# GpSimd's gathers of source nodes in a graph layer: the loop with staged index copies against 160 chunks written out

## The reference, cut to what matters

```python
seg = lambda v: jax.ops.segment_sum(v, dst, num_segments=n)
xs = x[src]
deg_w = jnp.maximum(seg(edge_weights), 1.0)
deg_c = jnp.maximum(seg(jnp.ones_like(edge_weights)), 1.0)
norm = edge_weights / jnp.sqrt(deg_w[src] * deg_w[dst])
gcn = seg(norm[:, None] * xs) @ Wgcn + bgcn
sage = x @ Wsage_s + seg(xs) / deg_c[:, None] @ Wsage_n + bsage
agg_w = seg(edge_weights[:, None] * xs)
gin = ((1.0 + gin_eps) * x + agg_w) @ Wgin + bgin
gconv = x @ Wgc1 + agg_w @ Wgc2 + bgc
eop = seg(edge_weights[:, None] * jax.nn.relu(xs + edge_attr)) @ Wedge + bedge
ops = jnp.stack([gcn, sage, gin, gconv, eop])
...
x = _layernorm(x + jnp.einsum('k,knd->nd', weights, ops), axis=-1)
```

## Time and profile before

| | us |
|---|---|
| median of 3 runs | 2110.08 |
| lowest and highest run | 2105.61, 2110.34 |
| span of the profiled execution | 2149.6 |

### The profile page before, as it was taken

How to read it: one execution, slowest core, us unless ns; L and a number is a source line. 1 busy time by engine, 2 the same in 40 slices (tenths; PEclk the granted TensorE clock), 3 DMA queues, 4 the chain that set the end, 5 groups by cost and what they waited for, 6 DMA issues and landing times.

```text
span 2149.6 us, 24142 instructions
## 1 busy us (share of the span) xinstructions
PE 1612.0 (75%) x6229; PEld 1037.0 (48%) x6229; DVE 949.9 (44%) x2579; ACT 868.5 (40%) x1181; POOL 1416.1 (66%) x1730
## 2 busy tenths in 40 slices
PE   2006577688889888888888988978988888888435
PEld 1005567545445454555455545545545455445335
DVE  7882465534334343443244433433435253334325
ACT  3784333334434252543254433533435253344003
POOL 6673766676676667667767666666666666666761
PEclk9999865889999899999899998989989999999757
DMA  5111433322222222222222222221222222212421
GB/s 98 25 25 46 132 106 100 83 44 47 58 51 61 48 47 58 52 48 58 44 66 49 55 60 44 54 51 43 68 48 47 54 57 47 59 43 56 103 44 37
DMA packets 81242, 124.52 MB, mean 58 GB/s; under 512 B 28856, under 2 KB 30631, under 8 KB 80009
## 3 DMA queue, kind: packets, MB, share of 16 engines
q0 software_dynamic: 44544, 48.32, 13.4%
q1 hardware_dynamic: 34966, 74.37, 10.9%
q10 hardware_dynamic: 1650, 1.04, 0.2%
HBM read 120.23 MB, written 3.40 MB: 58 GB/s over the span
## 4 chain that ended last, share of the span: by engine, by line
PE 40%; issue 20%; another core or an unknown queue 17%; DVE 11%; ACT 6%; POOL 3%; DVEq 2%; DMA 0%; POOLq 0%; SPq 0%; ACTq 0%
PE psum L1276 26%; PE psum L1257 11%; ACT ring L606 4%; POOL ring L564 3%; DVE ring L1072 2%; DVE sums L1061 2%; DVE early L986 1%; ACT early_x L687 1%; DVE attr L951 1%; DVE early L990 1%; PE psum L1308 1%; PE psum L1337 1%; PE psum L1338 1%; DVEq L1061 1%
## 5 line engine op out<-in xcount | busy, mean ns | idle before, releaser
L564 POOL DMA_INDIRECT ring<-node_table,idx x1280 | 1239.5, 968 | 612.4 <-issue 505.3
L1276 PE MATMUL psum<-table_sb,early_x 128*128 128x455 f32 x2464 | 1040.0, 572 | 46.5 <-issue 33.3
L1276 PEld LDWEIGHTS psum<-table_sb,early_x 128*128 128x128 f32 x2464 | 479.4, 200 | 531.2 <-issue 516.4
L1257 PE MATMUL psum<-ring 128*128 128x120 f32 x2560 | 412.5, 316 | 225.2 <-DVE ring L1072 104.7
L1257 PEld LDWEIGHTS psum<-ring 128*128 128x128 f32 x2560 | 378.3, 226 | 289.8 <-issue 160.1
L687 ACT ACTIVATE early_x<-early,minus_ids 128x256 f32<-128x256 f16 x616 | 408.1, 746 | 239.2 <-remote 144.6
L986 DVE TENSOR_TENSOR early<-psum,digit_hot 128x455 f32<-128x455 f32 x176 | 111.0, 631 | 885.4 <-remote 580.8
L678 ACT ACTIVATE early<-early 128x256 f32<-128x256 f32 x44 | 18.3, 416 | 523.4 <-DVE early L1007 305.0
L653 ACT ACTIVATE ring<-attr 128x512 f32<-128x512 f32 x160 | 99.6, 623 | 319.2 <-DVE attr L951 230.6
L690 ACT ACTIVATE early_x<-early_x,ones 128x1792 f32<-128x1792 f32 x88 | 157.4, 1789 | 2.9
L1257 PE MATMUL psum<-early 128*128 128x120 f32 x576 | 100.8, 328 | 75.8 <-issue 37.0
(11 more groups left out here) (156 smaller groups left out, 611.3 us busy)
## 6 DMA issues: line engine op xcount, KB each, us to landing
attr<-in_edge_attr SPq DMA_DIRECT2D x79, 512.0 KB
ring<-node_table,idx POOLq DMA_INDIRECT x1280
early<-in_edge_attr SPq DMA_DIRECT2D x36, 256.0 KB
src_all<-in_src SPq DMA_DIRECT2D x7, 1024.0 KB
early<-key_rows SPq DMA_DIRECT2D x11, 512.0 KB
early_x<-degree_rows SPq DMA_DIRECT2D x2, 1568.0 KB
early_x<-in_x,early_idx POOLq DMA_INDIRECT x112
node_table<-table_sb SPq DMA_DIRECT2D x1, 1666.0 KB, 6.1
```

Of the source, the lines that this page charges most:

```text
L564: nc.gpsimd.indirect_dma_start(out=feat[:, u, j, D:BLOCK], out_offset=None, in_=table, in_offset=bass.IndirectOffsetOnAxis(ap=idx[:, u, j: ...
L1257: last = nc.tensor.matmul(to[:, 0:3 * WINDOW], features[:, j, 0:2 * D], hots[:, j].rearrange("p k n -> p (k n)"), start=(j == 0), stop=(j ...
L1276: last = nc.tensor.matmul(pick_ps[k % 2].rearrange("p (b c) -> p b c", b=SPLIT), node_hot[:, k, a], table_sb[:, a * SPLIT:(a + 1) * SPLIT, ...
```

## The change

The loop over rounds becomes a Python loop over the 160 late chunks, so that the program holds every chunk's instructions in a row. Each gather names its own column of `e_src` directly. The tile `idx`, the 320 copies and the semaphore `staged` are gone. The wait for a slot's previous gathers is left out for the first four chunks, where it waited for 0. `gathers_begun` is raised once for each chunk. The other engines' programs are the same instructions with other line numbers.

```diff
-        idx = sb("idx", [P, UNROLL, TILES], U32)
-
...
-        staged = sem("staged")
...
                 pool.wait_ge(table_stored, 16)
-                with pool.Fori(0, LATE_STEPS) as i:
-                    for u in range(UNROLL):
-                        it = v * LATE + i * UNROLL + u
-                        pool.wait_ge(gathered[u], (v * LATE_STEPS + i) * (16 * TILES))
-                        for j in range(TILES):
-                            if j % HALF == 0:
-                                tiles = slice(j, j + HALF)
-                                nc.gpsimd.tensor_copy(idx[:, u, tiles], e_src[:, bass.ds(i * UNROLL + u + BASE, 1), tiles].rearrange("p c j -> p (c j)")).then_inc(staged, 1)
-                                pool.wait_ge(staged, it * 2 + j // HALF + 1)
-                                if j == 0:
-                                    pool.wait_ge(chunk_product, it + 1)
-                                pool.sem_inc(gathers_begun, 1)
-                            nc.gpsimd.indirect_dma_start(
-                                out=feat[:, u, j, D:BLOCK], out_offset=None, in_=table,
-                                in_offset=bass.IndirectOffsetOnAxis(ap=idx[:, u, j:j + 1], axis=0),
-                            ).then_inc(gathered[u], 16)
+                for c in range(LATE):
+                    u = c % UNROLL
+                    if c >= UNROLL:
+                        pool.wait_ge(gathered[u], (v * LATE_STEPS + c // UNROLL) * (16 * TILES))
+                    pool.wait_ge(chunk_product, v * LATE + c + 1)
+                    pool.sem_inc(gathers_begun, 1)
+                    for j in range(TILES):
+                        nc.gpsimd.indirect_dma_start(
+                            out=feat[:, u, j, D:BLOCK], out_offset=None, in_=table,
+                            in_offset=bass.IndirectOffsetOnAxis(ap=e_src[:, c + BASE, j:j + 1], axis=0),
+                        ).then_inc(gathered[u], 16)
```

## The result

The changed kernel takes 2156.12 us (median of four runs, 2154.0 to 2159.41); the kernel before, timed beside it, 2109.07. The ratio is 1.0228, with a 95% interval of 1.021 to 1.0246: **slower by 47 us**, where 38 us less were forecast.

What follows compares the result with a forecast made beforehand. TensorE's round with VectorE and ScalarE was taken to pace the profiled turns, GpSimd close behind and bounding the plain end. From 2110.1 us, 27.7 (24.3 + 3.4) and 10 came off: 2072.4 us, range 2025 to 2103.

Steps and rivals of the forecast that it cites:

- GpSimd's own cost of a turn: GpSimd's gathers without copies: a turn falls from 139.5 to 123 us, a chunk from 11.6 to 10.25 us.
- From the profiled execution to the timed ones: Timed turns take about 140.3 us, next to GpSimd's 139.5, so GpSimd paces at least quick ones; some 10 us gained.
- The turns: Eleven turns: GpSimd's 16.5 us saved a turn are hidden by TensorE's round at 143.9 us; worth nothing in the profiled execution.
- The plain end: Late chunks 152 to 159, bound by GpSimd: it starts at 2001.6 and ends at 2083.6 us, gaining 24.3 us.
- The factor load: Load of node factors in the plain end: holds gathers back from VectorE 20.72 us again, now at late chunk 153; no loss.
- The start of the turns: Late chunk 17: VectorE's wait of 3.43 us for gathers goes, 3.4 us gained.
- The turns are let go: Rival: GpSimd paces all timed turns, so each may fall to 135.4 us; 27.7 + 54 off, 2028 us; chance 0.26.
- Slower, by the clock: Rival: shifted work lowers TensorE's clock in the turns, some 10 us each; 2122 us with five such turns; slower: chance 0.06.
- By the code: Rival: reading in the straight program costs time, slower or level; chances 0.06 for slower, 0.08 for level.
- the gathers are not quicker: Rival: a gather indexed from the big table costs 0.17 us more, eating the 1.4 us a chunk; 2110 us; level: chance 0.08.
- The factor load takes the gain of the end: Rival: GpSimd stands still during the factor load in the plain end, losing 20.7 us; 2093 us; chance 0.10.

Runs made afterwards that it cites:

- again: The kernel before, unchanged, run once more for a profile: 2111.68 us, ratio 1.0001; profiled span 2104.2 us.
- late_paused: Changed kernel with an unused copy and its wait ahead of each four gathers from late chunk 4 on: 2129.88 us, ratio 1.0074.
- start_paused: Changed kernel with an unused copy and its wait ahead of each four gathers in late chunks 0 to 3 alone: 2142.70 us, ratio 1.0129.
- the execution shown ahead: The kernel before, unchanged, in the profile shown ahead of the prediction: span 2149.6 us.
- straight_copies: Kernel before with late gathers written out chunk by chunk, copies into the index tile and their waits kept: 2110.11 us, ratio 0.9998.
- dummy_copies: Changed kernel with an unused copy and its wait ahead of each four gathers throughout: 2112.64 us, ratio 1.0007.

## Why the prediction was wrong, point by point

- **GpSimd's own cost of a turn**: right. The unhindered chunks at the start take 9.98 us (10.25 forecast, from a mean gather that has the lengthened ones in it), with gaps of 0.30 us throughout, and GpSimd waits 20 us a turn under "remote" alone (221.6 in eleven turns), as named.
- **From the profiled execution to the timed ones**: right in its reading. In the timed runs the kernel before is paced by GpSimd: 140.5 us a turn in "again", 140.3 by the arithmetic, with 310 us of VectorE waiting for gathers. What was drawn from it was wrong.
- **The turns, the step that failed**: "What hides them is TensorE's round. In the profiled execution that is worth nothing", and 1 us a turn gained in the timed runs. TensorE's round was taken as fixed, some 135 to 144 us, whatever GpSimd did beside it. It is not: 110.5 us with four gathers a chunk or fewer, at most 140.5 with groups of four where GpSimd paces and 143 to 144 in the two profiles where it does not, 142.4 with unbroken ones. The change made GpSimd's part shorter (140.5 to 123), and the round of TensorE beside it was then longer than what GpSimd's part had been. The term was -10 us; measured, by the turns of the profiles, +20.5.
- **A stage that the sum left out**: the node products beside the first 32 gathers. No term stood for it, since nothing there waits for a gather. Measured +30 us at late chunk 0, of which some 15 to 21 us reach the end (late_paused is 15 us over the kernel before, start_paused 13 us under the changed one by its median of 2142.70, 21 by its ratio).
- **The plain end**, -24.3 us: the size was off. GpSimd's first gather for late chunk 152 came at 2020.60, not at 2001.6, and its last at 2108.60. The product of late chunk 148 that was to free the slot was itself late: TensorE was at it from 2004.56 to about 2013.6, with 1.5 to 1.7 us of idle "issue" between single instructions, and GpSimd's gather saw it 7 us later ("remote"). The end gained 9.9 us against "again", 3.2 against the execution shown ahead. The factor load did as forecast: VectorE waited 16.21 us, at late chunk 153.
- **The start of the turns**, -3.4 us: not seen; chunks 0 to 16 lost 6.4 us.
- **The rivals.** "The turns are let go" had the right picture of who paces them and missed for the same reason as the forecast. "Slower, by the clock" had the right sign, at a chance of 0.06. Its mechanism was not it: the mean clock of the whole changed kernel was 0.885 to 0.893 in its runs and 0.898 in "again", and TensorE's busy time of a turn did not rise. "By the code" and "the gathers are not quicker" are excluded by straight_copies and dummy_copies. "The factor load takes the gain of the end" did not come about: GpSimd went on issuing through it, without a pause from 2044.22 to 2099.
- **A small slip**: gathers of 968 ns on average for a median of 944 are 31 us over 1280 of them, not 28. No term used it.
- **What I could have read**: TensorE's idle time of 46.5 us before L1276, 33.3 of it "issue", and of 225 us before L1257 stood in the page of the kernel before, and the turns with the same work took 135 and 152 us. Both are marks of a round that something disturbs, and I took them for the clock. The groups of four disturbed it already.

What stays open is the path by which gathers reach TensorE. The records show its instructions stretched by idle time and its results taken late by others; they don't show what it lacks. One path that no run tests is that TensorE's own instructions come late: the page has two queues of the kind "instruction", and no view shows when they deliver. Nor is it settled whether gather instructions, their packets or GpSimd's time on them count, whether the length of a run or the share of breaks does, and why the kernel before took 2144.57 us beside some of the experiments.

## What to carry to other kernels

A wait that costs an engine time may be what keeps another engine running. Before taking a wait away from an engine that issues gathers, measure the others' round with most of the gathers left out: here it was 110 us under a pace of 140, and such a kernel is one run. And where a change makes one of two nearly equal engines quicker, the other's time is to be read from executions in which it is alone, not taken from those in which both run.

## What the runs showed of the hardware

- Unbroken indirect gathers of 0.94 us at a pitch of 1.25 us hold TensorE up after some ten of them: rounds of 2.45 us became 5 to 19 us. With breaks of 1.0 us every four gathers TensorE kept its pace there (late chunk 0 at 217 to 224 us in seven profiles, against 246 to 253 in ten without breaks). Breaks of 1.0 us every eight gave nothing there (246.3), of 1.5 us more (230.5, one profile).
- Inside a stretch that gathers disturb, single TensorE instructions start at multiples of 0.7 us after one another (125 of 129 in the changed kernel).
- The harm does not fall with the bytes (a third: 1.018) or the rows (half: 1.033); four gathers a chunk with a break of 4.4 us on average do none (110.4 us a turn). Every gather, of 128 rows or 64, of 272 bytes or 68, leaves 32 packets.
- A wait of GpSimd for a semaphore that it has just raised makes no gap (0.30 us as always); one for its own copy ahead of a gather makes one of 0.8 us, and between two copies 0.17 us.
- Plain copies on GpSimd (656 ns each) stretched a VectorE instruction with two SBUF inputs from 0.18 to 1.56 us on average and 5.33 at most. TensorE had no idle time without a cause beside them.
